# Probability tiles in a ring of eight, values visited in threes, and the FFN's absolute sums beside the grouped outputs

## What is computed

```python
x = x + xattn(layernorm(x), ctx)     # 16 heads over 1601 context rows, softmax; keys and values from a 32-wide latent
x = x + attn(layernorm(x), ...)      # 32 heads, 8 key heads of 128, 512 cached keys + the new ones, softmax, output weight
x = x + ffn(layernorm(x), ...)       # below
def _binary_diff_weight(w, base):    # for w1, w2, w3, each 1792 x 512
    d = w - base
    return base + mean(abs(d)) * sign(d)
h = silu(x @ W1.T) * (x @ W3.T);  out = h @ W2.T
```

## Time and profile before

| | us |
|---|---|
| three runs | 902.95, 906.02, 907.76; median 906.02 |
| the profiled execution's own time | 903.59 |
| its span, first to last instruction | 901.8 |
| mean granted TensorE clock | 0.987 of full |

### The profile page before, as it was taken

One profiled execution on the slowest core, in us unless ns is written; L12 is line 12 of the kernel. 1 busy time (PEld: TensorE's weight loads), 2 busy tenths in 40 slices (PEclk: granted clock), 3 DMA queues, 4 the chain that ended last, 5 costly groups with the idle time before them and its releaser, 6 DMA issues.

```text
span 901.8 us, 15515 instructions
## 1 busy us (share of the span) xinstructions
PE 861.6 (96%) x5402; PEld 654.4 (73%) x5402; DVE 609.3 (68%) x994; ACT 521.6 (58%) x1011; POOL 416.4 (46%) x272
## 2 busy tenths in 40 slices
PE   6899999999987979999999999999999999899998
PEld 4445555555532768888888888888888887788886
DVE  4865676577543448768587685876858769767784
ACT  4756666666675546546365463654636557555552
POOL 2597787778874024423244232442324525144430
PEclk9989999999998989999999999999999999999999
DMA  9947756532651522011020110201102004446521
GB/s 358 325 169 273 275 209 213 192 127 66 217 174 59 222 83 71 24 41 54 0 70 23 43 50 0 70 23 40 53 0 70 13 1 137 144 141 204 188 99 47
DMA packets 43202, 102.96 MB, mean 114 GB/s; under 512 B 7954, under 2 KB 13074, under 8 KB 42258
## 3 DMA queue, kind: packets, MB, share of 16 engines
q1 hardware_dynamic: 42866, 102.06, 33.0%
q10 hardware_dynamic: 288, 0.26, 0.1%
HBM read 96.95 MB, written 1.05 MB: 109 GB/s over the span
## 4 chain that ended last, share of the span: by engine, by line
PE 61%; DVE 2%; ACT 1%; DMA 1%; POOL 0%; SPq 0%; issue 0%
PE psum L1359 11%; PE psum L1345 10%; PE psum L1475 9%; PE psum L1413 8%; PE psum L1371 6%; PE psum L1489 4%; PE psum L1398 3%; PE psum L1389 3%; PE psum L1394 3%; PE psum L1380 1%; PE psum L1392 1%; PE psum L1390 1%; DMA ffn_raw<-in_L_ffn_mean_w_dram 1%; POOL ffn_quant L1860 0%; DVE x L1831 0%; DVE norm_stats L162 0%
## 5 line engine op out<-in xcount | busy, mean ns | idle before, releaser
L1847 POOL TENSOR_TENSOR head_probs<-head_probs,inverse_den 128x576 f32<-128x576 f32 x128 | 147.4, 1152 | 273.1 <-DVE inverse_den L1700 273.0
L982 DVE TENSOR_REDUCE max_part<-psum 128x1 f32<-128x804 f32 x128 | 121.0, 989 | 44.0 <-PE psum L694 43.9
L871 ACT ACTIVATE probs<-psum 128x512 f32<-128x512 f32 (+1 forms) x208 | 107.9, 601 | 54.7 <-PE psum L715 48.1
L1582 ACT ACTIVATE head_probs<-psum,neg_max 128x576 f32<-128x576 f32 x128 | 94.8, 741 | 51.1 <-DVE neg_max L1713 50.4
L555 POOL TENSOR_TENSOR prob_sums<-probs 128x1024 f32<-128x1024 f32 x48 | 114.2, 2389 | 18.7 <-ACT probs L871 9.8
L1713 DVE TENSOR_REDUCE neg_max<-psum 128x1 f32<-128x576 f32 x128 | 96.9, 757 | 23.8 <-PE psum L1359 22.6
L1359 PE MATMUL psum<-k_high,query_t_high 128*128 (+1 forms) x256 | 86.6, 338 | 2.0 <-DVE coeff L1786 2.0
L1693 DVE TENSOR_TENSOR probs_t_low<-psum,probs_t_high 128x512 fp32r<-128x512 f32 x124 | 84.8, 684 | 1.0
L715 PE MATMUL psum<-q_t,c_t 97*128 97x512 f32 (+1 forms) x208 | 73.7, 435 | 7.9 <-ACT probs L871 6.3
L1371 PE MATMUL psum<-ident,head_probs 128*128 128x128 f32 x496 | 77.9, 273 | 1.6 <-DVE query_t_low L1672 1.4
L694 PEld LDWEIGHTS psum<-c_t,q_t 96*128 96x128 f32 x256 | 43.6, 190 | 47.9 <-DVE max_part L982 25.1
(11 more groups left out here) (221 smaller groups left out, 1919.3 us busy)
## 6 DMA issues: line engine op xcount, KB each, us to landing
ctx_t_odd<-in_ctx_dram SPq DMA_DIRECT2D x4, 3202.0 KB, 10.7
w_raw<-in_L_ffn_w_dram SPq DMA_DIRECT2D x24, 448.0 KB, 5.1
w_raw<-in_L_ffn_mean_w_dram SPq DMA_DIRECT2D x24, 448.0 KB, 6.4
ffn_raw<-in_L_ffn_w_dram SPq DMA_DIRECT2D x42, 256.0 KB, 3.8
ffn_raw<-in_L_ffn_mean_w_dram SPq DMA_DIRECT2D x42, 256.0 KB, 4.3
cache<-in_ctx_dram SPq DMA_DIRECT2D x3, 3202.0 KB, 10.8
wq_nat<-in_L_attn_wq_dram SPq DMA_DIRECT2D x32, 256.0 KB, 3.0
wo_nat<-in_L_attn_wo_dram SPq DMA_DIRECT2D x32, 256.0 KB, 2.7
```

Source lines behind the costliest of these rows:

```text
L871: act.activation(prob_buffer(b, t)[0:rows, half * BANK:(half + 1) * BANK], psum[0:rows, n % SCORE_BANKS, :], ACT.Exp, scale=XSCALE).then_i ...
L982: dve.tensor_reduce(max_part[:, qt, pair:pair + 1], psum[:, bank:bank + 2, 0:PIECE_KEYS], AX.XY, ALU.max).then_inc(s_max, 1)
L1582: act.activation(probs[:, qt, :].rearrange("p (a k) -> p a k", a=2), psum[:, 2 * (qt % 2):2 * (qt % 2) + 2, 0:HALF], ACT.Exp, bias=neg_max ...
L1847: pool.tensor_tensor(probs[:, qt, :], probs[:, qt, :], rden[:, qt:qt + 1].to_broadcast([P, KEYS]), ALU.mult).then_inc(s["norm"], 1)
```

## The change

1. The ring `probs` has eight tiles instead of four; there are still six `prob_sums`.
2. POOL adds tiles into fewer, longer sums: three per step for batches 0 to 4 (tiles 0 to 3, 4 to 7, 8 to 12; ten additions), five for batches 5 and 6 (eight additions), seven for batch 7 (six additions).
3. `values` takes three units at a time: two visits in a step instead of six. The tail's two products stand in `tail_and_denominators`, beside the first sum's two. With three sums that is 2 groups of four products where there was one of two and three of four.
4. The maxima stand otherwise: three of them in a row (13, 14, 15) after the second visit.
5. The copy of the values' result, and the placing of the next values, can now start only after the tail, at the very end of the step.
6. The pass over the FFN's weights moves to the attention: pieces of 1/7, in `head(g, 0)` for g = 1 to 7. POOL subtracts beside `output` once `values_low` is done, ACT sums the absolute values at the end of `head(g, 0)`, after `output_weight_high(g, 0)`, and SP loads the pieces one g ahead. `coeff` is now made in head 30. POOL's difference for FFN chunk 0 moves ahead of the heads.

```diff
+STEADY = ((0, 1, 2, 3), (4, 5, 6, 7), (8, 9, 10, 11, 12))
+FEWER = ((0, 1, 2), (3, 4, 5), (6, 7), (8, 9), (10, 11, 12))
+FEWEST = ((0, 1, 2), (3, 4), (5, 6), (7, 8), (9, 10), (11,), (12,))
+GROUPED = (STEADY,) * (BATCH - 3) + (FEWER, FEWER, FEWEST)
...
-    probs = [core.sb(f"probs{i}", [P, XQ], ctx=own) for i in range(4)]
+    probs = [core.sb(f"probs{i}", [P, XQ], ctx=own) for i in range(RING)]
...
+                pe.wait_ge(s_exp, HALVES * (b + 1))
+                pe.wait_ge(s_add, adds_through(b, parts[0][-1]))
+                for half in range(2):
+                    at = 2 * LKV * half
+                    mm = pe.matmul(psum[at:at + LKV, U_BANK, :], c_nat[0:TAIL, b % 3, KT - 1, :],
+                                   prob_buffer(b, KT - 1)[0:TAIL, half * BANK:(half + 1) * BANK], start=False, stop=True)
+                    add_up(0, 1, half)
+                mm.then_inc(s_pv, 1)
...
-                abs_sum(b, 1)
-                abs_sum(b, 2)
...
+                    if i == 1:
+                        sp.wait_ge(s_abs, 3 * (g - 1) + 1)
+                        for k in range(3):
+                            for j, n in enumerate(wnames[k]):
+                                sp.dma_start(pieces[k][:, j, :], flat[n][:, bass.ds((g - 1) * PIECE, PIECE)]
+                                             ).then_inc(s_piece[k], 16)
...
-            pe.wait_ge(s_co, 1)
             run(pe, head)
...
+                if last and i == 0:
+                    for k in range(3):
+                        abs_sum(g, k)
+
+            def abs_sum(g, k):
+
+                if k == 0:
+                    act.wait_ge(s_tot, g)
+                act.wait_ge(s_pdiff, 3 * (g - 1) + k + 1)
+                act.activation(pieces[k][:, 0, :], pieces[k][:, 0, :], ACT.Abs,
+                               accum_out=part[:, k:k + 1]).then_inc(s_abs, 1)
...
+                if i == 0 and last:
+                    pool.wait_ge(s["vl"], 2 * g + 2)
+                    for k in range(3):
+                        pool.wait_ge(s_piece[k], 32 * g)
+                        pool.tensor_tensor(pieces[k][:, 0, :], pieces[k][:, 0, :], pieces[k][:, 1, :],
+                                           ALU.subtract).then_inc(s_pdiff, 1)
```

More of the change, by code:

```diff
@@ L327, with adds_of, adds_before, adds_through @@
 C_WIDTH = MAIN + TAIL
-DIFF_AT = (0, 1, 2)
-ABS_AT = 3
+STEADY = ((0, 1, 2, 3), (4, 5, 6, 7), (8, 9, 10, 11, 12))
+FEWER = ((0, 1, 2), (3, 4, 5), (6, 7), (8, 9), (10, 11, 12))
+FEWEST = ((0, 1, 2), (3, 4), (5, 6), (7, 8), (9, 10), (11,), (12,))
+GROUPED = (STEADY,) * (BATCH - 3) + (FEWER, FEWER, FEWEST)
+def adds_of(b):
+    return [(t, n, t == tiles[1]) for n, tiles in enumerate(GROUPED[b]) for t in tiles[1:]]
+def adds_before(b):
+    return sum(len(adds_of(i)) for i in range(b))
+def adds_through(b, t):
+    done = [i + 1 for i, (at, n, first) in enumerate(adds_of(b)) if t == at or (first and t == GROUPED[b][n][0])]
+    return adds_before(b) + done[0] if done else 0
+def sum_number(b, n):
+    return sum(1 for i in range(b) for tiles in GROUPED[i] if len(tiles) > 1) + n
 COMPRESS_BANK = (4, 3, 6) + (4,) * (BATCH - 3)
@@ L371, in cross_attention @@
     max_part = core.sb("max_part", [P, QTILES, PAIRS], ctx=own)
-    probs = [core.sb(f"probs{i}", [P, XQ], ctx=own) for i in range(4)]
-    sums = [core.sb(f"prob_sums{i}", [P, XQ], ctx=own) for i in range(ADDS)]
+    sums = [core.sb(f"prob_sums{i}", [P, XQ], ctx=own) for i in range(SUMS)]
+    probs = [core.sb(f"probs{i}", [P, XQ], ctx=own) for i in range(RING)]
     u_all = core.sb("u_all", [P, 2, BANK], ctx=own)
@@ L412, in cross_attention @@
     s_idx = core.sem("index_in", own)
-    s_raw = [core.sem(f"w_raw_in{i}", own) for i in range(3)]
-    s_diff = core.sem("w_diff_done", own)
-    s_abs = core.sem("w_abs_done", own)
     s_c = core.sem("compressed", own)
@@ L521, in _ @@
             sp.dma_start(index[:, :], arg["block_idx"].rearrange("(a k) -> a k", a=1)).then_inc(s_idx, 16)
-            for i in range(3):
-                load_pieces(0, i)
             place_keys(1)
@@ L825, in _, with maximum @@
                 lead = b + 1 < BATCH
[L826 to L829 removed]
+                def maximum(i):
                     if lead:
[L831 to L847 removed]
+                        max_scores(b + 1, i)
+                maximum(0)
+                scores(b, 2)
+                if b == 0:
+                    maximum(1)
+                    compress(2)
+                scores(b, 3)
+                if b > 0:
+                    maximum(1)
+                    mix(b - 1)
+                maximum(2)
+                if b == 0:
+                    natural(2)
+                scores(b, 4)
+                maximum(3)
+                scores(b, 5)
+                maximum(4)
+                scores(b, 6)
+                maximum(5)
+                values(b, range(0, 3))
+                for t in range(7, KT):
+                    maximum(t - 1)
+                    scores(b, t)
+                maximum(KT - 1)
+                values(b, range(3, 6))
+                maximum(KT)
+                maximum(KT + 1)
+                maximum(KT + 2)
                 if b + 3 < BATCH:
@@ L1264, in attention_and_ffn @@
     total = core.sb("abs_total", [P, 3], ctx=own)
+    part = core.sb("abs_part", [P, 3], ctx=own)
+    pieces = [over(f"w_piece{k}", [P, 2, PIECE], F32, "cache", 8 * k * PIECE) for k in range(2)]
+    pieces.append(core.sb("w_piece2", [P, 2, PIECE], ctx=own))
+    s_piece = [core.sem(f"w_piece_in{k}", own) for k in range(3)]
+    s_pdiff = core.sem("w_piece_diff_done", own)
+    s_abs = core.sem("w_piece_abs_done", own)
     coeff = core.sb("coeff", [P, 3], ctx=own)
@@ L1354, in score @@
                     pe.wait_ge(s["ql"], n + 1)
+                if isinstance(g, int) and n == NH - 2 and qt == 1:
+                    pe.wait_ge(s_tot, NKV)
+                    pe.matmul(psum[:, 3, HALF:HALF + 3], ones[:, :], total[:, :], start=True, stop=True).then_inc(s_all, 1)
+                elif isinstance(g, int) and n == NH - 2 and qt == 3:
+                    pe.wait_ge(s_co, 1)
                 for half in range(2):
@@ L1848, in head @@
                                        ALU.mult).then_inc(s["norm"], 1)
+                if i == 1 and last and not (isinstance(g, int) and g == 0):
+                    pool.wait_ge(s_abs, 3 * g + 1)
+                    pool.tensor_tensor(total[:, :], total[:, :], part[:, :], ALU.add).then_inc(s_tot, 1)
                 if i == 0:
```

186 lines of the change are left out of this document (76 added, 110 removed).

## The result

| | before | after |
|---|---|---|
| median of four runs, us | 905.42 (902.95 to 907.76) | 928.90 (926.96 to 930.67) |
| profiled execution's own time, us | 903.59 | 930.28 |
| its span, us, and mean granted clock | 901.8, 0.987 | 928.2, 0.978 |

The ratio is 1.0259, 95% interval 1.0221 to 1.0297: 2.6% slower. 932 was forecast, 914 to 944 as the range.

What follows compares the result with a forecast made beforehand. PE's queue was taken to bound the cross attention and the attention. 903.59 + 3.0 (cross attention) + 23.5 (attention) = 930.1 us; with the median 2.4 above the profiled execution, 932, range 914 to 944 (8 in 10).

Steps and rivals of the forecast that it cites:

- Fewer visits, by PE's own queue: Cross attention, steps 1 to 4: fewer value visits, tail's own visit and one denominator group gone save PE 3.2 us a step.
- What waits instead: Cross attention, steps 1 to 4: new PE waits of 3.5 us against 3.2 saved, +0.25 a step, +1.0 for four.
- The wait for mix's bank and the pace of maxima 4 and 5: Cross-attention steps: maximum 3 waits for DVE's `update_x`, then maxima 4 and 5 go at DVE's pace, 0.55 us.
- Steps 5 and 6: Cross attention without compression: the turning waits for all 16 maxima, +4.4 us for both steps, plus 1.7 for one half clock.
- Steps 0 and 7: Cross attention's ends: step 0 no longer waits for POOL, -1.6 us; step 7 loses its 1.98 wait and half clock, -2.5.
- The absolute sums: Attention: ACT's three sums behind the weight copy delay PE's transpose by 2.2 us in each of seven groups, 15.4 us.
- Half clock in the attention: Attention: PE's 2.0 us waits bring half clock, 1.7 us each in five groups of seven, 8.5 us.
- Rival 1: Whole kernel: same waits but the clock stays up, without 8.5 and 1.7 us; 922 us, chance 0.25.
- Rival 2: Whole kernel: PE's queue sum decides, waits are smaller, and ACT's sums vanish in the head's slack; 886 us, chance 0.06.
- Rival 4: Attention: SP's piece loads delay query weights, PE waits 2 to 4 us more in seven groups; 946 to 960 us, chance 0.07.
- Rival 5: Whole kernel: the sums overlap the outputs and waits cancel the visits, so nothing changes; 903 to 909 us, chance 0.04.
- Rival 3: Cross attention gains 1.5 us in each of steps 1 to 6, attention loses 23.5; 916 us, chance 0.14.

Runs made afterwards that it cites:

- the five products: Kernel after with five idle 512-column products behind the turning, ahead of the first scores of cross-attention steps 6 and 7: 928.44 us.
- the kernel with products on both sides: Kernel after with idle products around the turnings that end cross-attention steps 5 and 6, three ahead and five behind: 924.47 us.
- the first experiment: Cross attention of the kernel before, without its FFN differences, with the output stage of the kernel after: 919.31 us, ratio to before 1.0134.
- the early sums: Kernel after with two absolute sums of a group ahead of the weight copy and the third in the next head: 911.40 us.

## Why the prediction was right, and where only its sum was

932 against 928.9. The waits came where they were forecast, in both stages. Their sizes did not add up as forecast: the profiled execution is 26.7 us longer where 26.5 was the sum, but of it the cross attention has 9.96 (forecast 3.0) and the rest 16.7 (23.5). That these two misses of 7 us cancel is luck. By its own steps:

- **Fewer visits, by PE's own queue.** 3.2 us of PE's time were to go from a step; its busy time fell by 1.69. The tail's own visit went (forecast 1.0, measured 1.07), and so did one group of the denominators: from their start to the next maximum 0 it is 1.86 us with the tail in it, where it was 2.71 (0.85, forecast 0.86). The term that failed is 0.34 for a visit. Its 0.14 held: the value products take 5.85 us a step in six visits, 5.42 in two and 5.57 in three. The 0.20 for the maxima and steps beside a visit did not come, so four visits less gave 0.43 and not 1.36. Of these 2.3 us, ACT's pace between the visits took back 0.65. The Trainium skill says in "TensorEngine Tiling (Array Packing)", section Key Properties, that changing the tiling mode drains the engine. The 0.15 for a visit agrees with some such price; no run here shows whether it is that. The 1.07 of the tail's visit is none, since it is the time of its own group.
- **What waits instead.** 3.5 us forecast, 2.18 more idle time measured. Most places were right: 0.98 of waits ahead of the compression (forecast 1.35), 0.70 ahead of the scores (0.63), 0.69 for exponentials at the step's start, where mix now comes 0.38 later (0.3). The 0.65 for tiles at ACT's pace fits what PE's busy time hides: by the starts of their records, scores and maxima take 15.0 us in a step of after, idle time left out, and 14.4 in before. The wait for mix's bank and the pace of maxima 4 and 5 (together 0.55) is not in the timeline. The change in busy and in idle time was thus each put 1.3 to 1.5 too large, with opposite signs: +0.25 forecast, +0.49 measured. The net was luck to that extent.
- **Steps 5 and 6.** +4.4 of waits and +1.7 of half clock forecast, +9.1 measured. The waits were 1.38 and 1.20 as walked (1.6 and 1.2). I charged one half clock of 1.7; both steps had one, and each cost more. From the turning to the next maximum 0 they take 9.02 and 8.80, against 6.61 where the clock stayed up (with the five products in the wait): 4.6 for both. That is the term that was mis-sized, by about 3.
- **Steps 0 and 7.** -1.6 forecast, -1.75 measured, and -2.5 in the kernel with products on both sides, whose queue is the same up to there. Step 7: -2.5 forecast, +0.24 measured. The wait of 1.98 is gone, as the old cross attention without differences also shows, but half clock came back behind a wait of 1.07 and in the last visits: a visit of twelve value products (24 records) took 3.71 and 4.15 us, where it takes 2.78 in step 2. Cross attention in all +3.0 forecast, +9.96 measured in the profile, and some +7.3 by the first experiment (9.6 by the medians, less the 2.3 that the missing differences gave in its profile).
- **The absolute sums.** 2.2 us of wait and shift in each of seven groups: 2.04 to 2.06 waited, the groups' period 58.37 instead of 56.24, +2.13. That nothing in a head gives it back was right, and doubled sums come through one for one.
- **Half clock in the attention.** 8.5 us for five groups of seven; it came once, at 638.31, where the next wait is 59.96 later instead of 58.37: 1.6 us. This step failed, by 7 us, and it failed in the other direction than the one in steps 5 and 6, so that the sum stood. I had two waits of 1.97 and 1.98 and made a rule of them. Seven more of 2.05 gave one half clock here, and seven in the 42 such waits of all six kernels that have them (two in the kernel with the old cross attention and the late sums, one in each other). Two closer together of 1.38 and 1.20 gave it both times.

The granted clock at that one place in after:

```profile
638.00:642.00 4.00, 3.69 (x21) 3.48 (x22) 2.90 (x7) 3.20 (x10) 2.26 (x2) 0.70 0.00 0
```

Rival 1 (clock stays up, 922) was nearly right in the attention and wrong in the cross attention. Rival 2 (the queue's sum) is refuted in both halves: PE's busy time fell by half of its 3.2, the waits took all of that, and the sums did not vanish in the head. Rival 4 (late pieces) did not come: the early sums need them sooner still and wait for nothing but POOL. Rival 5 (903 to 909) is out by 20 us. Rival 3 (a gain in the cross attention) did not come. With smaller visits and the maxima spread a steady step is 0.68 shorter than before, but half clock at the end takes that back: the last mix starts at 286.75, against 284.26 in before.

## What to carry to other kernels

A piece of background work costs by its place in an engine's queue first. In the wrong place its whole length came through, one for one; in the right one none of it did. Look for where that engine waits already (ACT waited 10.35 us right ahead of the three sums) and put it before the instruction that ends the wait, not behind. If a change gathers one kind of work on an engine to save switches, walk the other engines' pace past the gathered block: what is drawn together leaves them idle, and what follows it then comes at their pace. When the wait that follows stands next to another one, splitting them with useful work may be worth more than the work costs, as the clock counts too: here it went well at five turnings of six. And read PE's busy time with care: products that wait for a bank between their records can stand in it as work.

## What the chip showed that I had not expected

- Half clock depends on more than one wait's length. In these traces it came behind a wait of 5.16 us at all seven, close behind 2.05 at seven of 42, and behind 1.29 to 1.38 and then 1.20, with 1.1 us of short transposes between them, at ten turnings of ten (in some it began over the transposes). With a visit of 1.05 in the place of the second wait it came at one of six.
- The same instructions in the same order on PE differ by 3 us at the end of the cross attention (291.47, 292.00, 294.22, 294.65 in four kernels that differ only behind it). The Trainium skill, "TensorE: Matmul & The Clock Gate", section Part 1: The HAM clock gate, says that the activity monitor runs free of the kernel's start, so that the same kernel can meet it in another phase. The spread agrees; no run here shows the phase itself.
- Two visits of twelve value products and three of eight differ by 0.15 us a step in the products' own time and by nothing in PE's busy time, but the tail's two products cost 1.07 us in a visit of their own, and nothing in the group of the first sum.
- What stays open: why the half clock in the kernel with products on both sides of the turning still came, and whether a longer filling would hold it off.
